# A graph layer on one NeuronCore: the units' one-hots made by ScalarE in two passes instead of by VectorE in one

## The reference

```python
hs, hd = h[src], h[dst]
e = concatenate([hs, hd], axis=1)
a_k = exp(relu(e @ W_att_k + b_att_k))                 # k = 1, 2, 3
att_k = segment_sum(a_k, dst)
avg_a = (a1 / att1[dst] + a2 / att2[dst] + a3 / att3[dst]) / 3
m = avg_a * relu(relu(relu(hs @ W1 + b1) @ W2 + b2) @ W3 + b3)
h_neigh = segment_sum(m, dst) / maximum(deg, 1)
out = relu(concatenate([h, h_neigh], axis=1) @ W_c1 + b_c1) @ W_c2 + b_c2
result = layernorm(h + out)
```

## Time and profile before

| | before |
|---|---|
| median of 3 runs | 774.49 us (770.85 to 776.41) |
| the profiled execution | 772.04 us |
| its span, first to last instruction | 767.9 us |
| mean granted clock of PE | 0.864 |
| busy, share of the span | PE 85%, DVE 77%, POOL 72%, ACT 63% |
| L1428, gathers | 526 instructions, 511.8 us busy |
| L2036, one-hot by DVE | 49 instructions |
| L1753 and L1755, one-hot by ACT | 93 instructions each |

### The profile page before, as it was taken

The page is one execution under the profiler, slowest core; times in us unless marked ns, Lnnn a source line. Parts: engine busy times, 40 slices in busy tenths (PEclk is TensorE's granted clock), DMA queues, the critical chain, the costliest instruction groups (busy, mean ns, idle before and its releaser), DMA issues.

```text
span 767.9 us, 17623 instructions
## 1 busy us (share of the span) xinstructions
PE 651.9 (85%) x5388; PEld 535.7 (70%) x5388; DVE 593.9 (77%) x1881; ACT 486.6 (63%) x1128; POOL 553.2 (72%) x576
## 2 busy tenths in 40 slices
PE   8962679898879957789999999999988888888785
PEld 5752457765656633469999999999977777777664
DVE  4883577989777969877888888888765778777776
ACT  5554776877665536557777777777565555655563
POOL 7677777777777775467777777777777777777760
PEclk9985597879797776659999999999989788989797
DMA  7984353433883323223333333333352444445431
GB/s 224 258 207 105 67 80 82 97 81 79 77 71 86 67 59 88 46 56 72 82 79 81 79 81 80 82 82 79 76 137 65 107 131 107 118 105 136 101 95 34
DMA packets 81572, 73.70 MB, mean 96 GB/s; under 512 B 34056, under 2 KB 65472, under 8 KB 81472
## 3 DMA queue, kind: packets, MB, share of 16 engines
q0 software_dynamic: 18112, 37.94, 25.3%
q1 hardware_dynamic: 63072, 34.43, 16.8%
q10 hardware_dynamic: 288, 0.13, 0.1%
HBM read 62.91 MB, written 9.52 MB: 94 GB/s over the span
## 4 chain that ended last, share of the span: by engine, by line
PE 43%; POOL 22%; DVE 13%; issue 12%; ACT 6%; DMA 2%; DVEq 1%; SPq 0%; ACTq 0%
POOL work L1428 22%; PE bank L1660 15%; PE bank L1615 9%; PE bank L1641 3%; PE bank L1621 3%; DVE counts L1940 3%; DVE acc L1925 2%; DVE acc L2128 2%; ACT acc L1777 2%; PE bank L646 2%; PE bank L667 2%; PE bank L1567 1%; DMA work<-message_table,src_t 1%; PE bank L655 1%; PE bank L1572 1%
## 5 line engine op out<-in xcount | busy, mean ns | idle before, releaser
L1428 POOL DMA_INDIRECT work<-message_table,src_t x526 | 511.8, 973 | 178.4 <-issue 155.9
L1615 PE MATMUL bank<-work 128*128 128x144 f32 (+7 forms) x1132 | 175.8, 310 | 24.0 <-DVE acc L2128 23.9
L1615 PEld LDWEIGHTS bank<-work 128*128 128x128 f32 x1132 | 163.6, 220 | 33.8 <-issue 19.3
L1803 ACT COPY work<-bank 128x192 f32<-128x192 f32 (+5 forms) x120 | 36.0, 300 | 183.1 <-DVE work L2078 181.0
L2128 DVE TENSOR_TENSOR acc<-acc,bank 128x192 f32 (+7 forms) x283 | 85.9, 303 | 27.0 <-issue 4.4
L1660 PE MATMUL bank<-shared,acc 128*128 128x129 f32 (+1 forms) x784 | 95.6, 275 | 0.0
L2109 DVE TENSOR_TENSOR work<-bank,work 128x576 f32<-128x576 f32 (+5 forms) x120 | 83.5, 696 | 12.5
L1660 PEld LDWEIGHTS bank<-shared,acc 128*128 128x128 f32 (+1 forms) x784 | 91.5, 192 | 0.0
L1641 PE MATMUL bank<-acc 128*128 128x294 bf16 (+3 forms) x240 | 64.4, 406 | 29.6 <-ACT acc L1782 20.9
L1940 DVE TENSOR_TENSOR counts<-counts,bank 128x294 f32 (+3 forms) x120 | 68.9, 574 | 11.4 <-issue 7.5
L1641 PEld LDWEIGHTS bank<-acc 128*128 128x128 bf16 x240 | 23.1, 113 | 69.5 <-ACT acc L1782 36.5
(11 more groups left out here) (188 smaller groups left out, 999.6 us busy)
## 6 DMA issues: line engine op xcount, KB each, us to landing
work<-message_table,src_t POOLq DMA_INDIRECT x526
side<-near_nodes SPq DMA_DIRECT2D x97, 48.0 KB
side<-logit_parts SPq DMA_DIRECT2D x283, 0.8 KB
message_table<-work SPq DMA_DIRECT2D x12, 262.0 KB, 4.5
work<-message_table SPq DMA_DIRECT2D x48, 65.5 KB, 1.8
work<-in_x_t SPq DMA_DIRECT2D x12, 256.0 KB, 4.2
counts<-in_x SPq DMA_DIRECT2D x11, 256.0 KB, 3.4
logits_or_x<-in_x_t SPq DMA_DIRECT2D x11, 256.0 KB
```

The lines of the kernel that those rows point to most:

```text
L1428: pool.indirect_dma_start(out=rows_of(n)[:, t, :], out_offset=None, in_=table[:, :], in_offset=bass.IndirectOffsetOnAxis(ap=src_t[:, h, g: ...
L1615: pe.matmul(sums[:, at:at + HEADS * w], rows_here[:, t, 0:P], wt_of(i)[:, t, :], start=h == 0, stop=h == TILES - 1)
```

## The change

`by_dve` is true for units 0 to 2 only, and no longer for all units below 27. For units 3 to 26 DVE's `one_hot` is left out of its loop, and ACT's `one_hot`, which returned at once for them, makes the two passes at its place in ACT's loop. PE waits for these units on ACT's semaphore. Nothing else changes.

```diff
             def by_dve(i):
 
-                return first and i < HOT_AT
+                return first and i < AHEAD
```

## The result

The changed kernel takes 788.62 us (median of 4 runs, 786.79 to 791.32) against 773.4 us (4 runs, the three of the table ahead and one more, 770.85 to 776.41): a ratio of 1.0198 with an interval of 1.0145 to 1.0251, slower by about 15 us. The forecast was 792.0 with a range of 781 to 804, and slower.

What follows compares the result with a forecast made beforehand. The counting stage, bound by a loop of waits through all engines, delays the gathers one for one. Loop +18.3, before step 4 +0.6, VectorE's relief -1.0 make +17.9 us: 789.9 profiled, plus 2.45 for the median, 792; range 781 to 804.

Steps and rivals of the forecast that it cites:

- Part A: Steps 4 to 16, ScalarE from early-row copy through the odd step's low one-hots; six predicted at 56.68 us together.
- Part B: Steps 4 to 16, from those one-hots over TensorE to the next copy; larger of 9.89 us and old value, 67.99 together.
- The pair of passes: ScalarE's two one-hot instructions for a half pass, priced at 1.37 us, 2.74 us for a long unit.
- Before step 4: Early counting stage: the step 2 pass partly hidden by a wait, +0.6 us; passes of steps 0 and 1 hidden.
- After step 16: Late counting stage: ScalarE's waits for mask copies hide the 12.3 us of passes in steps 17 to 23; cost 0.
- What DVE gives back: Steps 19 to 23: three of five passes taken off VectorE credited at 0.336 us each, -1.0 us.
- From the last stall on: Sign: the length from the gathers' last stall to the end stays unchanged.
- Clock: Rival: TensorE's clock falls in the loop, B 13.54 us in all six pairs, +13.3 us, 805 us; chance 0.11.
- DVE's relief: Rival: ScalarE's added work hides and half of VectorE's 43 passes were on the path, 767 us; chance 0.04.
- Cancel: Rival: ScalarE's waits in B hide more and VectorE's earlier sums shorten slow B parts, 774 us; chance 0.08.
- series: Rival: all 43 pairs of ScalarE instructions end up in series, costing 58.9 us, 833 us; chance 0.03.
- the early pairs: Sign: in the loop of early-row copies, the early pairs of steps (14.23 us before) lengthen most, pairs nearing 20 us.

Runs made afterwards that it cites:

- e1: Kernel before, but ScalarE makes the one-hots of units 3 to 19, VectorE those of units 20 to 26; 792.65 us, ratio 1.0277.
- e3: Kernel before, but ScalarE makes the one-hots of odd units 3 to 19, in even steps behind the early-row copy; 791.28 us, ratio 1.0253.
- e4: Kernel before, but ScalarE makes the one-hots of even units 4 to 18, in the odd steps; 779.82 us, ratio 1.0122.
- e9: Kernel before, with the second L1984 of a step moved behind add_sums on VectorE; 780.95 us, ratio 1.0123.
- e10: Kernel before, with L1984 reading one operand instead of two, a maximum left out for two heads; 766.10 us, ratio 0.9939.
- e2: Kernel before, but ScalarE makes the one-hots of units 20 to 26, VectorE all earlier ones; 771.22 us, ratio 1.0001.
- e5: Kernel before, with VectorE's pass of units 3 to 26 on one column and distances capped at 0; 768.73 us, ratio 0.9999.
- e12: Changed kernel with even-step passes ahead of the early-row copy, plus one-operand L1984, a maximum left out for two heads; 787.63 us, ratio 1.0200 to the kernel before.
- e6: Changed kernel with the even step's pass ahead of the early-row copy; 789.29 us, ratio 1.0284 to the kernel before.

## Why the prediction was right

**The bound and its price.** The counting stage sets the end: delay 19.9, additional stalls 20.4 us. This mechanism is the prediction's, and it held.

**Part A** came to 56.18 us for 56.68. e1 and e3 repeat it within 0.03. All of the even steps' passes is on the path, except what waits in front of the mask copy; those waits went as the prediction had it. The half microsecond is the second pair (9.10 for 9.60), where such a wait of 0.28 us was overlooked in the kernel before:

```profile
141.19 0.32 ACT L1803 COPY work<-bank 128x192 f32<-128x192 f32 x1 [0.28 <-DVE work L2078]
```

**Part B** came to 69.29 for 67.99, and that closeness is partly luck: e1 has the same work in this loop and came to 65.70. The reason is only half right, too. I let each pair be the larger of ScalarE's floor and the old value. The floor shows (9.71 in the first pair for 9.89), but the other pairs are not the old ones (11.91 for 10.45, 11.00 for 13.56). The parts B of after, one by one, with the columns of the earlier trace rows:

```profile
135.83:145.54 9.71, 8.56 (x76) 7.50 (x77) 6.27 (x21) 8.87 (x22) 7.55 (x8) 0.82 0.37 93
154.64:166.55 11.91, 11.86 (x76) 9.70 (x77) 6.82 (x21) 9.18 (x22) 9.17 (x10) 0.57 0.36 87
176.03:186.38 10.35, 7.75 (x76) 5.89 (x77) 6.92 (x20) 9.18 (x22) 7.91 (x9) 1.00 0.37 92
195.86:209.65 13.79, 13.73 (x75) 10.32 (x76) 7.16 (x22) 9.33 (x22) 4.67 (x5) 0.50 0.21 51
219.17:230.17 11.00, 10.95 (x76) 8.76 (x77) 6.36 (x18) 9.33 (x21) 2.66 (x4) 0.66 0.48 60
239.68:252.21 12.53, 9.84 (x75) 6.27 (x76) 7.28 (x21) 9.21 (x22) 5.93 (x7) 0.80 0.82 89
```

Pairs 2 to 5 go with the clock: with about the same matmuls, B is 10.35 us at the full clock, and 11.00, 11.91 and 13.79 at 0.66, 0.57 and 0.50; in these three PE is busy almost all the time (13.73 of 13.79 us in the slowest). The sixth, 12.53, doesn't fit: PE is idle for 2.7 us of it, of which the late early rows, 3.64 us in the kernel before, make only 0.59. The rest stays open. What the odd steps' passes cost is thus no fixed 3.4 us: B grew by 1.1 in e1, 4.7 in after and 7.2 in e4.

**The pair of passes.** In after the first pair begins at 127.22 and the second at 128.60, 1.38 us apart for the 1.37 of the sum. The estimate of 1.23 that I worked out from the Trainium skill ("ScalarE: Activation LUTs", section What ACT_TABLE_LOAD costs) is too low here; the second instruction waits for the first.

**Before step 4, +0.6.** Measured +0.65 from step 0 to 4, which is luck: e9 and e10 have the same work there as before (38.75 us) and took 36.07 and 41.53. **After step 16, 0.** e2 costs nothing, and the waits shrank by 11.8 us. **What DVE gives back, -1.0.** Between the copies of steps 16 and 18 0.94 us went, but in e5 a relief of 5.9 us was worth nothing that can be measured; I count this term as not shown.

**From the last stall on "unchanged".** 395.13 for 396.72 us, true here, but not a rule: e1, e3 and e9 give 400 to 405 by the holds, of which the prediction knew nothing.

**The sum.** On the profiled executions +17.9 was forecast and 19.3 came. On the medians it is +15.2: the runs of after spread over 4.5 us and the profiled one is the longest, while that of before lies below its median. So the forecast of 792 was right in its mechanism and its size, but that it is within 4 us of the median owes something to luck.

**The rivals.** *Clock*: in part. The clock fell from 0.84 to 0.76 in the stretch from 105 to 235 us, and three parts B were long by it; but the old values in the sum held slow steps too, and how much of B is new was not separated. The 805 us did not come, since five of the six pairs still had at least one step with sums of 1.90 us. The Trainium skill ("TensorE: Matmul & The Clock Gate", Part 1), where gaps bring the lower level back, agrees in direction: the clock fell where TensorE did fewer matmuls in the same time (770 for 848). e12, slow in one step of each pair, is the nearest thing to this rival. *DVE's relief*: fallen, since ACT's work in A does not hide (e1, e3), and e5 shows no gain from 5.9 of the 14.4 us. *Cancel* and *series*: fallen by the loop's 125.47 us and by e2.

Two signs were missed. ScalarE was busy 88% and not "above 90%" from 105 to 235 us: its waits in front of the copy stayed at 0.7 to 3.9 us. And the early pairs are not those that lengthened most: the fourth did, by 7.1 us (16.17 to 23.27), the first by 4.6; the fourth is the one whose part B ran at a clock of 0.50.

## What to carry to other kernels

Where no engine is full, price a move between engines by the loop of waits: mark a turn of the loop by one instruction, split the turn where the path changes its engine, and put the added work into the part it stands in; the average shares said that ScalarE had 25% to spare, and there was almost none where the pass had to stand. An engine relieved beside the path need not give anything back (5.9 us taken off VectorE in e5, none seen in the time, within about 3 us). Before a gain of some us in one profiled loop is believed, look at the medians: with the same order of work, two loops differed by 8 us here as TensorE's clock went.

## What the runs showed of the hardware

- A gather on POOL is held by VectorE: started while an L1984 runs, which reads and writes SBUF alone (0.74 us with two operands, 0.48 with one), it ends 0.82 us after that instruction instead of 0.94 after its own start. The gathers lost 10.5 us by longer times in the hot stage of the kernel before and 18.9 in e9, and beside the 0.48 us instructions only 3.8 in e10.
- The loss can lock in. In the kernel before three gathers of 1.25 us with 0.5 us of hold make 4.25 us, one step of the hot stage, so the next gather meets L1984 again (354.69, 358.91, 363.18); in e9 thirteen gathers of 1.3 us or more, from 378.33 to 429.85, follow each other at 4.2 to 4.5 us. e1 and e3 change the counting stage alone and have 33 and 35 gathers above 1.1 us where before has 21; what sets the number was not tested.
- TensorE's clock can settle into a pattern with the loop: in e12 its sums alternated between 3.1 to 3.6 and 1.9 us through the whole loop (granted clock 0.72 from 105 to 235 us), in e6 with the same order they did not (0.78).
